# Reordering the swap of output weights in a chunked state-space kernel with a high/low split matmul

## The reference, cut to what matters

```
proj = xn @ in_proj_w.T                   # gate 8192, conv input 10240, dt 128
hBC  = silu(causal_conv4(conv part))      # hs (128 heads x 64), B, C (8 groups x 128)
dt   = clip(softplus(dt + dt_bias)); A = -exp(A_log)
# per chunk of 128 tokens and head: Y = ((C B^T) * decay) @ (hs dt) + exp(cum) C @ state + D hs
g    = Y * silu(gate)
out  = group_norm(g, 8 groups) * norm_w   # rms over 1024 channels
attn = out @ out_proj_w.T
ffn  = base + top-2 LoRA experts
result = x + attn + ffn
```

## Time and profile before

| what | value |
| --- | --- |
| median of 3 runs | 1772.38 us (1767.21 to 1773.53) |
| profiled execution, its time | 1772.65 us |
| its span | 1771.3 us |
| granted TensorE clock, mean | 0.985 |
| PE busy | 1654.7 us, 93% |
| PEld busy | 1309.2 us, 74% |
| DVE busy | 1395.9 us, 79% |
| ACT busy | 1224.5 us, 69% |
| POOL busy | 1313.9 us, 74% |
| DMA queue 1, share of 16 engines | 50.5% |

### The profile page before, as it was taken

How to read it: one execution, slowest core, us unless ns; L and a number is a source line. 1 busy time by engine, 2 the same in 40 slices (tenths; PEclk the granted TensorE clock), 3 DMA queues, 4 the chain that set the end, 5 groups by cost and what they waited for, 6 DMA issues and landing times.

```text
span 1771.3 us, 31672 instructions
## 1 busy us (share of the span) xinstructions
PE 1654.7 (93%) x10764; PEld 1309.2 (74%) x10764; DVE 1395.9 (79%) x1669; ACT 1224.5 (69%) x2630; POOL 1313.9 (74%) x1225
## 2 busy tenths in 40 slices
PE   6989989999998999989899998989999998999987
PEld 5777868777787777767687776867777676877766
DVE  5868778787888878787787877888788887878675
ACT  5167777776767767777677776777767777676764
POOL 2047678886788777886788767887688876887776
PEclk9999999999999999999999999999999999999999
DMA  3243356554555555553565437545565535654453
GB/s 123 74 168 100 113 185 159 161 159 113 190 163 164 135 149 165 158 168 113 168 181 174 136 111 191 168 152 144 155 170 154 180 102 165 179 161 147 133 159 102
DMA packets 232527, 265.46 MB, mean 150 GB/s; under 512 B 156072, under 2 KB 157616, under 8 KB 228144
## 3 DMA queue, kind: packets, MB, share of 16 engines
q1 hardware_dynamic: 232368, 263.45, 50.5%
HBM read 162.20 MB, written 69.73 MB: 131 GB/s over the span
## 4 chain that ended last, share of the span: by engine, by line
PE 50%; ACT 20%; DVE 16%; issue 12%; POOL 1%; ACTq 0%; DMA 0%; SPq 0%; DVEq 0%; POOLq 0%
PE P L245 15%; PE P L247 14%; PE P L246 14%; ACT P L534 7%; DVE hsX L728 7%; PE P L431 4%; DVE yb L981 2%; DVE P L978 2%; ACT hsX L473 2%; ACT OH L703 2%; ACT GH L505 1%; PE P L448 1%; ACT th L491 1%; DVE hsX L757 1%; ACT tg L706 1%
## 5 line engine op out<-in xcount | busy, mean ns | idle before, releaser
L687 ACT ACTIVATE sq<-yb 128x512 bf16<-128x512 f32 x128 | 80.8, 632 | 411.8 <-DVE yb L981 411.8
L534 ACT ACTIVATE P<-AB,SC 128x128 f32<-128x128 f32 x1024 | 308.5, 366 | 0.5 <-DVE hsX L739 0.5
L245 PE MATMUL P<-xh,AH 128*128 128x512 f32 x656 | 270.4, 412 | 1.4 <-DVE xl L822 1.4
L1010 POOL TENSOR_TENSOR AL<-AR,AH 128x512 fp32r<-128x512 f32 x82 | 109.7, 1338 | 218.0 <-ACT AH L460 218.0
L728 DVE SCALAR_TENSOR_TENSOR hsX<-P,cwt,hsX 128x1023 f32<-128x1023 f32 x189 | 242.1, 1281 | 36.3 <-ACT hsX L473 31.8
L247 PE MATMUL P<-xh,AL 128*128 128x512 f32 x656 | 258.4, 394 | 0.0
L246 PE MATMUL P<-xl,AH 128*128 128x512 f32 x656 | 257.1, 392 | 0.0
L245 PE MATMUL P<-GH,xh 128*128 128x512 f32 x544 | 217.9, 400 | 5.1 <-POOL GL L1015 5.0
L245 PE MATMUL P<-OH,gTh 128*128 128x512 f32 x512 | 217.0, 424 | 4.3 <-DVE OL L751 2.3
L1092 POOL TENSOR_TENSOR yb<-yb,dhs 128x512 f32<-128x512 f32 x112 | 143.7, 1283 | 103.6 <-DVE yb L952 103.2
L791 DVE TENSOR_TENSOR EM<-P,Gt 128x1024 f32<-128x1024 f32 x128 | 155.8, 1217 | 76.2 <-ACT P L539 68.0
(11 more groups left out here) (188 smaller groups left out, 4072.2 us busy)
## 6 DMA issues: line engine op xcount, KB each, us to landing
AB<-acr_d SPq DMA_DIRECT2D x128, 512.0 KB, 4.9
half_d<-hsX SPq DMA_DIRECT2D x60, 512.0 KB, 3.6
AR<-in_wa SPq DMA_DIRECT2D x80, 256.0 KB, 2.8
TS<-in_wg SPq DMA_DIRECT2D x16, 1024.0 KB, 5.1
TS<-in_wo SPq DMA_DIRECT2D x16, 1024.0 KB, 6.1
part_d<-pl SPq DMA_DIRECT2D x64, 256.0 KB, 3.1
pl<-part_d SPq DMA_DIRECT2D x64, 256.0 KB, 2.6
al<-acc_d SPq DMA_DIRECT2D x64, 256.0 KB, 3.0
```

What stands on the lines that cost most here:

```text
L245: te.matmul(o, ah_, bh_, start=(first and i == 0), stop=False)
L534: r = se.activation(E[:, h, :], AB[m % 2][:, h, :], ACT.Relu, bias=SC[s % 2][:, c, 3, h:h + 1], scale=-1.0)
```

## The change

Five things change; the number of matmuls stays.

1. PE issues the passes that need a low part of the weights (or of the state) last. In GT all eight matmuls with GH come first, then the four with GL. In O all eight with OH, then OL in the order 0, 1, 3, 2. In Off and St the two with the high part first, and only then the wait for the low part.
2. ACT's four copies into OH in c = 0 move from ahead of tanh and of the high part of GTr to behind them. The first of the four is now number 3, a plain copy of TS[3].
3. TS[3] is scaled in place by POOL at the start of c = 0 (a new instruction, which waits for the transfer of the weights), and its low part is made by POOL near the end of c = 0, behind the norm's small ops and ahead of the low halves and the projection's low part. DVE makes only three of four low parts: 0 and 1 in c = 0, now behind `gTl`, and 2 in c = 1.
4. Further order on ACT and DVE. In c = 0 the first tap goes ahead of the eight relus. In c = 7 exp goes ahead of the last two gate copies. The output copies (L692, L697) go ahead of the square (L687). On DVE, in slots in which a new tile is tapped, the decay product goes behind the copy of O (L993).
5. SP loads the next gate weights in c = 2 instead of c = 1.

The diff, cut to its core:

```diff
@@ PE, pe_gate(m)
             for k in range(4):
+                te.wait_ge(s_gh, 4 * (1 + s) + k + 1)
+                te.matmul(o, xh[:, k, tok(c)], GH[:, k, :], start=k == 0, stop=False)
+                te.matmul(o, xl[:, k, tok(c)], GH[:, k, :], start=False, stop=False)
+            for k in range(4):
                 te.wait_ge(s_gl, 4 * (1 + s) + k + 1)
-                r = mm3(o, [(xh[:, k, tok(c)], xl[:, k, tok(c)], GH[:, k, :], GL[:, k, :])], first=k == 0, last=k == 3)
+                r = te.matmul(o, xh[:, k, tok(c)], GL[:, k, :], start=False, stop=k == 3)
@@ PE, Off; St is changed alike, with BH, BL, DH, DL
+                        te.wait_ge(s_sh, n0(m))
+                        o = bank("Off", m)
+                        te.matmul(o, CH[:, tok(c)], SH[:, :], start=True, stop=False)
+                        te.matmul(o, CL[:, tok(c)], SH[:, :], start=False, stop=False)
                         te.wait_ge(s_sl, n0(m))
-                        mm3(bank("Off", m), [(CH[:, tok(c)], CL[:, tok(c)], SH[:, :], SL[:, :])]).then_inc(s_off, 1)
+                        te.matmul(o, CH[:, tok(c)], SL[:, :], start=False, stop=True).then_inc(s_off, 1)
@@ PE, O
+                    te.wait_ge(s_oh, 4 * so + 4)
                     for k in range(4):
-                        te.wait_ge(s_ol, 4 * ((m - 1) // 8) + k + 1)
-                        r = mm3(bank("O", m - 1), [(gTh[:, k, :], gTl[:, k, :], OH[:, k, :], OL[:, k, :])],
-                                first=k == 0, last=k == 3)
+                        te.matmul(o, gTh[:, k, :], OH[:, k, :], start=k == 0, stop=False)
+                        te.matmul(o, gTl[:, k, :], OH[:, k, :], start=False, stop=False)
+                    for k in (0, 1, 3, 2):
+                        if k == 3:
+                            te.wait_ge(s_olp, so + 1)
+                        else:
+                            te.wait_ge(s_ol, 3 * so + k + 1)
+                        r = te.matmul(o, gTh[:, k, :], OL[:, k, :], start=False, stop=k == 2)
@@ ACT
-                    act_relus(m + 1)
-                if m < M:
+                if m < M and c == 0:
                     for i in done:
                         act_tap(i)
                 if m + 1 < M:
+                    act_relus(m + 1)
+                if m < M and c:
+                    for i in done:
+                        act_tap(i)
+                if m + 1 < M:
+                    act_exp(m + 1)
                     if new_gate:
                         act_gate_hi(s + 1, (2, 3))
-                    act_exp(m + 1)
                     act_state_hi(m + 1)
-                if m < M:
-                    se.wait_ge(s_g, m + 1)
...
-                    se.activation(sq[:, :], yb[:, :], ACT.Square, accum_out=sqs[:, s % 2, c:c + 1]).then_inc(s_sq, 1)
                 if m and ps % 2 == 0:
...
-                if m < M and c == 0:
-                    se.wait_ge(ts_in, 16 * (3 + 2 * s))
+                if m < M:
+                    se.wait_ge(s_g, m + 1)
...
-                    for j in range(4):
-                        se.activation(OH[:, j, :], TS[:, j, :], ACT.Copy, scale=nwt[:, 4 * s + j:4 * s + j + 1]).then_inc(s_oh, 1)
+                    se.activation(sq[:, :], yb[:, :], ACT.Square, accum_out=sqs[:, s % 2, c:c + 1]).then_inc(s_sq, 1)
@@ ACT, behind tanh of GT(m + 1) and the high part of GTr(m)
+                    if c == 0:
+                        se.wait_ge(s_ts3, s + 1)
+                        se.wait_ge(ts_in, 16 * (3 + 2 * s))
+                        if m:
+                            se.wait_ge(s_o, m)
+                        se.activation(OH[:, 3, :], TS[:, 3, :], ACT.Copy).then_inc(s_oh, 1)
+                        for j in range(3):
+                            se.activation(OH[:, j, :], TS[:, j, :], ACT.Copy, scale=nwt[:, 4 * s + j:4 * s + j + 1]).then_inc(s_oh, 1)
@@ DVE, in c == 1, and behind L981
-                        dve_output_lo(s, (2, 3))
+                        dve_output_lo(s, (2,))
-                    if new_tiles:
-                        if m + 1 < M:
-                            dve_decay(m + 1)
@@ DVE, behind the copy of O (L993)
                 if m + 1 < M:
+                    if new_tiles:
+                        dve_decay(m + 1)
                     dve_gate(m + 1)
                 if m < M:
-                    if c == 0:
-                        dve_output_lo(s, (0, 1))
                     ve.wait_ge(s_gth, m + 1)
                     ve.tensor_tensor(gTl[:, :, :], bank("GTr", m).rearrange("p (k t) -> p k t", k=4),
                                      as_f(gTh[:, :, :]), ALU.subtract).then_inc(s_gtl, 1)
+                    if c == 0:
+                        dve_output_lo(s, (0, 1))
@@ POOL, behind pool_scaled(m + 1), and near the end of the slot
+                    if c == 0:
+                        pe_.wait_ge(ts_in, 16 * (3 + 2 * s))
+                        pe_.tensor_tensor(TS[:, 3, :], TS[:, 3, :], nwt[:, 4 * s + 3:4 * s + 4].broadcast_to([128, 512]),
+                                          ALU.mult).then_inc(s_ts3, 1)
...
+                    if c == 0:
+                        pe_.wait_ge(s_oh, 4 * s + 1)
+                        pe_.tensor_tensor(OL[:, 3, :], TS[:, 3, :], as_f(OH[:, 3, :]), ALU.subtract).then_inc(s_olp, 1)
@@ SP
-                    if c == 1 and s + 1 < NS:
-                        sp.wait_ge(s_ol, 4 * s + 4)
+                    if c == 2 and s + 1 < NS:
+                        sp.wait_ge(s_ol, 3 * s + 3)
+                        sp.wait_ge(s_olp, s + 1)
                         sp.dma_start(TS[:, :, :], wg[s + 1]).then_inc(ts_in, 16)
```

More of the change, by code:

```diff
@@ L211, in mamba_moe_block_kernel @@
             sem(n) for n in ("stp", "st_", "offp", "t1", "tpl", "yp", "t2", "g_", "op", "pl_", "plr", "alo", "al_", "oh_", "ol_"))
+        s_ts3, s_olp = sem("ts3"), sem("olp")
         te, se, ve, pe_, sp = nc.tensor, nc.scalar, nc.vector, nc.gpsimd, nc.sync
@@ L421, in pe_program @@
                         te.wait_ge(s_bl, ngc(m))
+                        te.wait_ge(s_dh, n7(m))
+                        o = bank("St", m)
+                        te.matmul(o, BH[:, c, :], DH[:, :], start=True, stop=False)
+                        te.matmul(o, BL[:, c, :], DH[:, :], start=False, stop=False)
                         te.wait_ge(s_dl, n7(m))
-                        mm3(bank("St", m), [(BH[:, c, :], BL[:, c, :], DH[:, :], DL[:, :])]).then_inc(s_stp, 1)
+                        te.matmul(o, BH[:, c, :], DL[:, :], start=False, stop=True).then_inc(s_stp, 1)
                     banks_free("Y", m)
@@ L436, in pe_program @@
                     te.wait_ge(s_gtl, m)
+                    so = (m - 1) // 8
+                    o = bank("O", m - 1)
+                    te.wait_ge(s_oh, 4 * so + 4)
                     for k in range(4):
-                        te.wait_ge(s_ol, 4 * ((m - 1) // 8) + k + 1)
-                        r = mm3(bank("O", m - 1), [(gTh[:, k, :], gTl[:, k, :], OH[:, k, :], OL[:, k, :])],
-                                first=k == 0, last=k == 3)
+                        te.matmul(o, gTh[:, k, :], OH[:, k, :], start=k == 0, stop=False)
[6 more added lines that the diff above has]
+                        r = te.matmul(o, gTh[:, k, :], OL[:, k, :], start=False, stop=k == 2)
                     r.then_inc(s_o, 1)
@@ L676, in act_program @@
                 if m + 1 < M:
+                    act_relus(m + 1)
[4 more added lines that the diff above has]
+                    act_exp(m + 1)
                     if new_gate:
                         act_gate_hi(s + 1, (2, 3))
-                    act_exp(m + 1)
                     act_state_hi(m + 1)
-                if m < M:
-                    se.wait_ge(s_g, m + 1)
-                    if s >= 2:
-                        se.wait_ge(s_rst, 8 * ((s - 2) // 2) + c + 1)
-                    if m:
-                        se.wait_ge(s_sq, m)
-                    se.activation(sq[:, :], yb[:, :], ACT.Square, accum_out=sqs[:, s % 2, c:c + 1]).then_inc(s_sq, 1)
                 if m and ps % 2 == 0:
@@ L697, in act_program @@
                     se.activation(pl[pc % 2][:, :], pl[pc % 2][:, :], ACT.Copy, scale=rst[:, pc, 1:2]).then_inc(s_plr, 1)
-                if m < M and c == 0:
-                    se.wait_ge(ts_in, 16 * (3 + 2 * s))
+                if m < M:
+                    se.wait_ge(s_g, m + 1)
+                    if s >= 2:
+                        se.wait_ge(s_rst, 8 * ((s - 2) // 2) + c + 1)
                     if m:
-                        se.wait_ge(s_o, m)
-                    for j in range(4):
-                        se.activation(OH[:, j, :], TS[:, j, :], ACT.Copy, scale=nwt[:, 4 * s + j:4 * s + j + 1]).then_inc(s_oh, 1)
+                        se.wait_ge(s_sq, m)
+                    se.activation(sq[:, :], yb[:, :], ACT.Square, accum_out=sqs[:, s % 2, c:c + 1]).then_inc(s_sq, 1)
                 if m + 1 < M:
@@ L749, in dve_output_lo @@
             for j in js:
```

(13 more changed lines are left out.)

## The result

The changed kernel takes 1677.65 us (median of 4 runs, 1676.24 to 1679.57), the one before 1772.16 on the same chip (1767.21 to 1773.53). The ratio is 0.947, with a 95% interval of 0.945 to 0.949: 94.5 us less. The span fell from 1771.3 to 1678.3 us, and the mean granted clock rose from 0.985 to 0.997 of 2.4 GHz.

A forecast was written before the change was run, and what follows sets the result against it. PE's matmuls bound ordinary slots; in c = 1 the swap stalled PE. Gains of 58.8 + 5 + 13.3 + 11 = 88 us from 1772.65 gave 1684.6, stated as 1684, own range 1671 to 1699, 80% range with rivals 1663 to 1715.

The forecast's parts named there:

- Slot c = 1: Moving the swap ends PE's waits at Off and St: 12.4 us even, 12.1 odd; 58.8 us over seven passes each.
- the step on O's bank: In c = 1, O wants BG's bank, free with the mask at 6.7 us after GTr's start; not late.
- Copy of O, EM: Copying O ahead of the square and EM removes BG's waits: 13.3 us, with 0.3 per pass left at even c = 0.
- Tap and exp: First tap before relus in c = 0 saves 8.1 us; exp before two gate copies in c = 7 saves 3.
- Low parts last: In GT, Off and St, GL waits mostly stay and nothing waited for SL, DL: zero, between -5 and +8 us.
- POOL takes an OL: One OL and a product on POOL in c = 0: taken as 0, up to 2.6 us per pass (42 us).
- First and last pass and the ends: Smaller stalls in the first and last pass, with 4 us of the gTl wait for both: 5 us gain taken.
- What would show it: Signs: gTl and tg waits under 3 us each, pl gone, al under 4, c = 1 at 12.1 to 12.4, ordinary slots unchanged.
- (1): DVE and POOL block each other, stretching OL and dxh: c = 1 takes 14.3 us, kernel 1715; chance 0.15.
- (2): All stalls go: c = 1 at 11.65 and 11.3 us, BG and GL waits gone, kernel 1663; chance 0.08.
- (4): No change: the stall moves whole from St to O because OL stays late; kernel 1770 us; chance 0.04.
- (3): Slower: POOL waits for output weights at the start of c = 0; 1819 us if landing 12 us later; chance 0.03.

The follow-up runs named there:

- e1: Kernel before with only the swap moved: OH copies behind the high part of GTr, OL 0 and 1 behind gTl; 1729.86 us, 0.9735 of before.
- e5: Changed kernel with the swap alone put back: OH copies ahead of tanh, OL 0 and 1 ahead of gTl; 1741.3 us, 0.981 of before.
- e4: Changed kernel with its other ACT and DVE reorderings undone (relus, gate copies, square, EM ahead again); 1720.82 us, 0.971 of before.
- e2: Changed kernel with PE's old matmul order in GT, O, Off and St; 1685.05 us, 0.9485 of before.
- v2: Changed kernel with DVE's copy of O ahead of the older tile's silu; 1688.72 us, 0.953 of before.
- e6: Changed kernel with only the relus back ahead of the first tap in c = 0; 1687.15 us, 0.953 of before.
- e3: Changed kernel with all four OL on DVE and nothing of the swap on POOL; 1677.28 us, 0.944 of before.
- v235_early_b: Changed kernel with copy of O before older silu, one GL on DVE, chunk 2's BH, CH, BL and mask early, OL 2 before state's sum; 1673.29 us, 0.9435.
- v235d_low_dve: v235_early_b with all four OL on DVE and nothing of the swap on POOL; 1670.96 us, 0.9416 of before.

## Why the prediction was right, point by point

The time was forecast as 1684 with an own range of 1671 to 1699, and is 1677.65. The sum was 88; by the spans it is 93.0. The mechanism held: the swap ahead of the gated rows was the large stall. That the sum came so near is partly luck. Three parts gained more than forecast, c = 1 by 3.0 us, the first and last pass by 3.2, tap and exp by 1.8, and an ordinary slot that it had unchanged lost 3.6. In c = 1 both slots lie outside the 12.1 to 12.4 that it gave as a sign.

- *Slot c = 1:* predicted 58.8, measured 7 x (5.35 + 3.48) = 61.8. The parts missed on both sides, 5.5 us and 3.9 us over seven slots, and the misses cancel in part. The odd slot was put at 12.1 and is 11.32, because my OL and dxh (1.27 and 1.16) were values between the stretched and the unstretched case, and its first two OL and dxh run unstretched (1.42 the pair, and 0.68). The even was put at 12.4 and is 12.96: there they are stretched. I wrote that O wants BG's bank "free with the mask at 6.7; not late"; the mask ends 7.3 after GTr's start at 1319.21, and O was ready for it 1.19 earlier. So the step on O's bank failed, by 0.6 us of DVE's time and by how early PE is there. e1 shows what the move of the swap was worth alone (46 us, 44.7 of them in c = 1), e5 that the stall comes back. The other 17 us of c = 1 need the other edits too: e4 gives 1.37 of the odd slot back.
- *Copy of O, EM:* predicted 13.3. Odd c = 7 and even c = 3, 5, 6 gained 0.88, 0.61, 0.61, 0.23 and even c = 0 lost 0.41: 7 x 1.92 = 13.4. The agreement hides two shifts: half of the odd c = 7's gain and all of even c = 0's loss are the matmul order's doing (e2). The 0.3 left for even c = 0 was 0.89, timelines of the kernel after, for PE and DVE:

```profile
1305.73 2.14 DVE L784 SCALAR_TENSOR_TENSOR hsX<-th,hsX 128x1024 f32<-128x1024 f32 x1
...
1307.80 0.74 DVE L1017 SCALAR_TENSOR_TENSOR al<-P,rst,al 128x512 f32<-128x512 f32 x1
...
1308.68 0.30 PE L313 MATMUL P<-ident,Bx 128*128 128x128 f32 x1 [0.89 <-DVE al L1017]
```

  The copy stands behind a silu that takes 2.14 us here beside POOL's last GL. The same silu in the kernel before took 1.22:

```profile
1378.15 1.22 DVE L757 SCALAR_TENSOR_TENSOR hsX<-th,hsX 128x1024 f32<-128x1024 f32 x1
```

  Its length alone doesn't set the wait: with PE's old order (e2) it takes 2.14 too and PE, which comes later, waits 0.43; with the other orders undone (e4) it takes 1.22 and PE waits 0.90. v2 took that wait away (0.89 shorter). That it was no gain there is the next stall's doing.
- *Tap and exp:* predicted 8.1 + 3, measured 7 x 1.43 = 10.0 and 7 x 0.42 = 2.9. e6 bears out the size (9.5), not the place: undone, most of it costs in odd c = 1. And even c = 7 keeps nothing of its 0.42 under PE's old order (e2: 11.73), so exp ahead pays only together with the low parts last.
- *Low parts last:* taken as 0 between -5 and +8. Undone (e2) the kernel is slower, by 7.4 us between chips and by 5.0 in the spans, so they gain about as much as the bound allowed. 7 x 0.91 = 6.4 is in c = 7, where I had booked it under the orders; 7 x 0.46 comes off again in even c = 0, and even c = 1 adds 7 x 0.21.
- *POOL takes an OL:* taken as 0, bounds 0 to 42. e3 says 0.4 us, which is nothing by its interval, with both parts present: relief of DVE and blocking of DVE. In v235_early_b it costs 2.3 against v235d_low_dve, with intervals that overlap a little.
- *SP's load in c = 2:* no such stall shows in the slots of after.
- *Unforeseen:* odd c = 2 is 0.51 longer, 3.6 us. I had ordinary slots unchanged, and had said that a longer one would mean a cost of the order of matmuls. It doesn't: with the old order (e2) the slot is 11.83 as well. Timelines of the kernel after, for DVE, POOL and PE:

```profile
1429.07 2.14 DVE L784 SCALAR_TENSOR_TENSOR hsX<-th,hsX 128x1024 f32<-128x1024 f32 x1
...
1430.09 2.04 POOL L1076 TENSOR_TENSOR S<-S,EA 128x512 f32<-128x512 f32 x1
...
1441.17 0.63 PE L469 MATMUL P<-ident,yb 128*128 128x128 f32 x4 [0.26 <-DVE yb L1008]
```

  POOL's state decay takes 2.04 beside the silu and 1.06 alone, a slot later (L1076 again at 1441.59). With no OL on POOL (e3) the silu took 1.69 and the slot 11.42. But POOL's OL is not the cause: e1 and v235d_low_dve have none on POOL either, and their odd c = 2 take 12.02 and 12.44, while e6 has it there and takes 11.32. The slot is longer where PE waits for `yb` at its end: 0.23 to 0.26 us after, 0.5 in e1, 0.9 in v235d_low_dve. What makes `yb` late there stays open.
- *First and last pass and the ends:* taken as 5, measured 8.2; no run splits it.
- *What would show it:* `gTl` under 3, `pl` gone, clock 1.00 in odd c = 1: as said. The waits of O for OL of 0.3 to 1 us in c = 1 did not come (in passes 1 to 14 there is none); the wait for the mask stands in their place. `tg` is 9.2, not under 3. I had put all 19.1 to the swap; seven waits of 1.4 were its doing and are gone, and the other ten, 9.2 us in both kernels, stand among the last eleven slots of the span. A look at where a group's waits lie, not only at their sum, would have told. `al` is 6.3, not under 4.
- *Rivals:* (1) DVE and POOL blocking each other is real, but what decides is where they lie. Ahead of O it touches only the seven even c = 1; in the odd ones OL 2 (1.83 us) and the silu (2.14) are stretched, and the slot is full of PE's work at 11.32 all the same. At 12.96 the even slot stayed just under the 13 that I had named as this rival's sign. The Trainium skill (SBUF — State Buffer, "SBUF: two separate sides") says that of such a pair whichever starts first has the shared port for its whole length and the other is blocked. The traces agree in that the same instruction is longer beside the other engine's and that the profile names no wait for it: dxh takes 0.68 alone and 1.76 beside POOL. (2) Not all stalls go: those for `al`, GL, the mask and `tg` are left, 30.9 us in sum. (4) falls with e1. (3) POOL waited 0.8 us in all for the output weights. Group by form in the kernel after, columns as in the earlier trace rows:

```profile
L1115 POOL TENSOR_TENSOR TS<-TS,nwt 128x512 f32<-128x512 f32 x16 | 17.1, 1068 | 0.8 <-DMA TS<-in_wo 0.8
```

## What to carry to other kernels

When one bank serves several producers, put work that isn't urgent (a swap of weights) behind the instruction that frees it, and then look for what frees the next bank: here it was the mask, behind a product that nobody waited for yet. Judge a move from DVE to POOL by how long DVE's other instructions take afterwards, not by the time of the one that is moved; one edit here took 16 instructions off DVE, left DVE's busy time as it was (1354.4 us without the edit, 1358.1 with it) and gained nothing. A part that gives 0.9 us a slot can cost 11 us in all if PE then waits longer at the next stall and the clock falls behind it, so run parts together with the one that removes the next stall.
